# Centroids as 64 more columns of the weights in the first stage, and the third norm's parts of five late products kept in memory

## The chip, the core and the metric

The kernel runs on one core of a Trainium2 chip. TensorE multiplies, VectorE, ScalarE and GpSimd (POOL in the rows) do elementwise work, SyncE (SP) issues most DMAs, and 16 DMA engines move the data. The metric is the device time of one execution in microseconds.

## The reference

x has 4 x 1024 tokens of 1024 numbers. The computation is a macaron block:

```
x = x + 0.5 * ffn(layernorm(x))
x = x + attention(layernorm(x))
x = x + 0.5 * ffn(layernorm(x))

ffn(y):  dots = softmax(y @ centroids.T / 0.1)        # 64 clusters
         hits = dots > 0.01
         dense = y @ weight.T + bias                   # 1024 x 1024
         out = where(any(hits, 1)[:, None] & any(hits, 0)[assignments][None, :], dense, 0)
```

Both ffn use the same weight, bias, centroids and assignments. The attention mixes, within each token, 32 query heads with 8 key and value heads of width 32.

## The kernel before

**Tiles and precision.** The 4096 tokens are 32 tiles of 128 (NT = 32), two tiles form a pair (NP = 16). Every operand of a product is split into a high part (fp32r) and a low part (what the rounding left), and a product is three matmuls for each of 8 blocks of 128 inner columns: high x high, high x low weight, low x high weight (`product`, L280). One half of the outputs, 512 columns, is thus 24 matmuls into one bank of the accumulation memory; each matmul has its own weight load, since the tokens are the stationary side:

```
pe.matmul(acc, hi[:, k, :], w_h[:, k, cols], start=(k == 0), stop=False)
pe.matmul(acc, hi[:, k, :], w_l[:, k, cols], start=False, stop=False)
last = pe.matmul(acc, lo[:, k, :], w_h[:, k, cols], start=False, stop=(k == KB - 1))
```

The order of work is written out by hand: each engine has one program, and semaphores join them.

**First stage** (to about 390 us). It computes the first ffn's dense outputs and the logits. Per tile: statistics on VectorE (`stats_first`), factors on GpSimd (`factors_first`), the normalised tile on ScalarE (`norm_first`, L742). From tile 4 on it is stored to memory (`store_normed`, L406) and loaded back in four block DMAs (`load_blocks`, L410), so that VectorE's 32 x 32 transposes turn it fully (`turn_first`, L984). ScalarE copies the high part (`high_first`, L751) and VectorE subtracts the low part (`low_first`, L988, semaphore `lo1`). TensorE then makes two halves a tile (`product_first`), and VectorE adds the bias into `f_out` (`read_first`, L1000). GpSimd masks tokens (`select_tokens`), and SP stores the tile.

The logits of a pair come from a product of their own, the other way round: the centroids are stationary, the tokens of both tiles are 256 moving columns (`pair_logits`, L295, 16 matmuls; `pair_first`, L1293). ScalarE copies the result (`copy_pair`), TensorE transposes it in two matmuls inside a later product (`fold_pair`, L1302), and VectorE adds its parts and makes the softmax (`pair_soft_in` L332, `pair_soft_out` L352, with the exponential on ScalarE between). TensorE's loop over the pairs 1 to 13 is: first half of tile 2p with the fold of pair p inside, second half, centroid product of pair p + 1, both halves of tile 2p + 1. Pairs 14 and 15 follow, and the mask of the output columns is made from all hits.

**Stage of attention** (to about 1010 us). Iteration i works on several tiles at once: projections of tile i - 1, scores of tile i - 2, heads of tile i - 3, the third norm of tile i - 4 with its transposes on TensorE, high copy (`high_third`, L874) and low part (`low_third`, L1112), and a half product of the second ffn. The parts of the third norm lie in the two sets `odd_hi` and `odd_lo`, even and odd tiles. The values of a tile are loaded into the first half of the tile `part` and transposed by VectorE into the other.

**Last stage** (from about 1012 us). The products of the 14 tiles in `LATE` (tile 31, then 5, 7, ... 29; v counts them) had no room in the stage before. Since their third norm's parts were overwritten, they are made again for each v: load of the tile, `norm_late` (L855), 8 transposes (`transpose_late`, L1393), `high_late`, `low_late`, and then two halves (`product_late`, L1401) into banks that alternate by v. VectorE reads each half under the masks (`read_late`), adds it (`add_late`), and between them finishes 18 tiles whose products were done earlier (`finish_ready`, L1202); from the fourth on these come through three slots by DMA (`load_stream`, L568) and a mask multiplication on GpSimd (L737).

## Time and profile before

| | us |
|---|---|
| three runs | 1194.28, 1195.89, 1196.83 |
| median of the runs | 1195.89 |
| the profiled execution, own time | 1196.15 |
| its span | 1194.3 |
| TensorE busy in the span | 1181.7 |
| VectorE, ScalarE, GpSimd busy | 799.3, 499.2, 441.0 |

The page counts busy time of each engine; matmuls are pipelined and their ends modelled, so the starts of TensorE's instructions tell more than their lengths. A row of a timeline has start, length, engine, line, operation, output and input, and in brackets the idle time ahead of it and who ended it. The clock granted to TensorE was full in all stretches.

### The profile page before, as it was taken

To read this page: it belongs to the slowest core of one execution; us is meant where nothing else is said; L and a number is where in the kernel's file an instruction comes from. 1 tells how busy PE (TensorE), PEld (TensorE's weight loads), DVE (VectorE), ACT (ScalarE), POOL (GpSimd) and SP (SyncE) were. 2 spreads that over 40 slices of the span, in tenths; PEclk is the share of its full clock that TensorE was granted. 3 is DMA by queue.
4 is the path that set the end of the run, shared out by engine and by line. 5 is a ranking of instruction groups with operands and counts; after the bars stand their busy time and mean duration, and the time that the engine had idled before them with its cause. 6 is when DMAs were issued, how large, how long until landed. Compare 5 with 4: busy or idle time off the path is not lost.

```text
span 1194.3 us, 24986 instructions
## 1 busy us (share of the span) xinstructions
PE 1181.7 (99%) x10072; PEld 1002.5 (84%) x10072; DVE 799.3 (67%) x1272; ACT 499.2 (42%) x718; POOL 441.0 (37%) x582
## 2 busy tenths in 40 slices
PE   7999999999999999999999999999999999999998
PEld 6888888888888888888888888888888878888887
DVE  6654554455444477787777877778777774199987
ACT  5232233222211355656656656565565663211110
POOL 1335445543424643433434334344343210051332
PEclk9999999999999999999999999999999999999999
DMA  8578777876565366565565666565655565017885
GB/s 275 144 206 232 207 206 193 225 211 182 164 189 159 98 169 169 148 171 146 160 166 139 181 152 152 160 155 164 161 142 164 129 169 193 2 72 259 279 304 195
DMA packets 344978, 208.73 MB, mean 175 GB/s; under 512 B 289440, under 2 KB 308640, under 8 KB 344864
## 3 DMA queue, kind: packets, MB, share of 16 engines
q1 hardware_dynamic: 329696, 187.73, 56.2%
q10 hardware_dynamic: 15168, 19.40, 4.7%
q8 instruction: 80, 1.31, 0.5%
q14 instruction: 34, 0.28, 0.1%
HBM read 118.49 MB, written 88.60 MB: 173 GB/s over the span
## 4 chain that ended last, share of the span: by engine, by line
PE 91%; DMA 3%; DVE 2%; issue 1%; ACT 1%; SPq 1%; POOL 1%; POOLq 0%; DVEq 0%
PE ps_b L285 9%; PE ps_q L285 8%; PE ps_q L287 8%; PE ps_q L286 8%; PE ps_b L287 8%; PE ps_b L286 8%; PE ps_a L285 8%; PE ps_a L287 8%; PE ps_a L286 8%; PE ps_t L292 6%; PE ps_q L1450 3%; PE ps_q L299 2%; PE ps_q L301 2%; PE ps_q L1425 2%; DMA y_scratch<-xa 1%
## 5 line engine op out<-in xcount | busy, mean ns | idle before, releaser
L318 POOL TENSOR_TENSOR var_eps<-moments,eps 128x1 f32<-128x1 f32 x96 | 18.2, 190 | 396.6 <-DVE moments L314 396.6
L285 PE MATMUL ps_a<-w_hi,odd_hi 128*128 128x512 f32 x368 | 147.7, 401 | 0.0
L287 PE MATMUL ps_a<-w_hi,odd_lo 128*128 128x512 f32 x368 | 143.8, 391 | 0.0
L286 PE MATMUL ps_a<-w_lo,odd_hi 128*128 128x512 f32 x368 | 143.2, 389 | 0.0
L635 POOL TENSOR_SCALAR f_out<-f_out,token_on 128x1024 f32<-128x1024 f32 x30 | 85.6, 2852 | 75.6 <-DVE f_out L1013 75.3
L686 POOL TENSOR_TENSOR x_ring<-x_ring,f_tmp 128x1024 f32<-128x1024 f32 x32 | 77.3, 2414 | 91.2 <-DVE best L1159 58.5
L285 PE MATMUL ps_b<-proj_hi,y_hi 128*128 128x512 f32 x256 | 103.3, 403 | 0.0
L287 PE MATMUL ps_b<-proj_hi,y_lo 128*128 128x512 f32 x256 | 100.0, 391 | 0.0
L286 PE MATMUL ps_b<-proj_lo,y_hi 128*128 128x512 f32 x256 | 99.7, 390 | 0.0
L327 ACT ACTIVATE y_tok<-x_ring,norms 128x1024 f32<-128x1024 f32 x64 | 79.7, 1245 | 38.0 <-ACT o_head L881 21.0
L737 POOL TENSOR_TENSOR late<-late,mask 128x1024 f32<-128x1024 f32 x18 | 44.1, 2463 | 137.3 <-DMA late<-x_scratch 91.6
L1120 DVE TENSOR_TENSOR y_lo<-ps_t,y_hi 128x1024 fp32r<-128x1024 f32 x32 | 39.2, 1224 | 76.1 <-ACT y_hi L900 76.1
L893 ACT COPY v_diag<-part 32x256 f32<-32x256 f32 x128 | 82.7, 646 | 1.1
L287 PEld LDWEIGHTS ps_a<-w_hi,odd_lo 128*128 128x128 f32 x368 | 69.1, 188 | 15.1
L286 PEld LDWEIGHTS ps_a<-w_lo,odd_hi 128*128 128x128 f32 x368 | 69.3, 188 | 13.1
L285 PEld LDWEIGHTS ps_a<-w_hi,odd_hi 128*128 128x128 f32 x368 | 69.2, 188 | 12.7
L285 PE MATMUL ps_q<-w_hi,odd_hi 128*128 128x512 f32 (+1 forms) x208 | 79.5, 382 | 0.0
L287 PE MATMUL ps_q<-w_hi,odd_lo 128*128 128x512 f32 (+1 forms) x208 | 79.3, 381 | 0.0
L286 PE MATMUL ps_q<-w_lo,odd_hi 128*128 128x512 f32 (+1 forms) x208 | 79.3, 381 | 0.0
L285 PE MATMUL ps_q<-proj_hi,y_hi 128*128 128x256 f32 x256 | 74.8, 292 | 0.0
L287 PE MATMUL ps_q<-proj_hi,y_lo 128*128 128x256 f32 x256 | 72.5, 283 | 0.0
L286 PE MATMUL ps_q<-proj_lo,y_hi 128*128 128x256 f32 x256 | 72.4, 283 | 0.0
(219 smaller groups left out, 3113.1 us busy)
## 6 DMA issues: line engine op xcount, KB each, us to landing
xa<-in_L_attn_x SPq DMA_DIRECT2D x32, 512.0 KB, 5.0
f_tmp<-f_scratch SPq DMA_DIRECT2D x32, 512.0 KB, 4.2
x_ring<-in_L_attn_x SPq DMA_DIRECT2D x32, 512.0 KB, 3.6
f_scratch<-f_out SPq DMA_DIRECT2D x30, 512.0 KB, 4.0
x_scratch<-x_ring SPq DMA_DIRECT2D x30, 512.0 KB, 3.5
y_scratch<-xa SPq DMA_DIRECT2D x28, 512.0 KB, 4.6
ya_tok<-y_scratch SPq DMA_DIRECT2D x112, 128.0 KB, 3.3
late<-x_scratch SPq DMA_DIRECT2D x22, 512.0 KB, 6.7
```

Of the source, the lines that this page charges most:

```text
L285: pe.matmul(acc, hi[:, k, :], w_h[:, k, cols], start=(k == 0), stop=False)
L286: pe.matmul(acc, hi[:, k, :], w_l[:, k, cols], start=False, stop=False)
L287: last = pe.matmul(acc, lo[:, k, :], w_h[:, k, cols], start=False, stop=(k == KB - 1))
L292: last = pe.transpose(ps_t[:, k, :], src[:, k * P:(k + 1) * P], ident[:, :])
L299: last = pe.matmul(pair_ps, cen[:, k, :], hi[:, k, :, :], start=(k == 0), stop=(k == KB - 1))
L327: return act.activation(y, x, ACT.Identity, bias=norms[of][:, t, 0:1], scale=norms[of][:, t, 1:2])
L635: pool.tensor_scalar(f_out[t % 2][:, :], f_out[t % 2][:, :], token_on[0][:, t:t + 1], None, ALU.mult).then_inc(f1_on, 1)
L686: pool.tensor_tensor(x_ring[t % RING][:, :], x_ring[t % RING][:, :], f_tmp[:, :], ALU.add).then_inc(x1, 1)
L737: pool.tensor_tensor(f[:, :], f[:, :], mask[:, :], ALU.mult).then_inc(s_masked, 1)
L893: last = act.copy(v_diag[rows, :].rearrange("p (k q g c) -> p q k g c", k=R4, g=HKV, c=T4)[:, :, :, :, c], v_cols[rows, :].rearrange("p (q ...
L1120: dve.tensor_tensor(y2_lo[:, :, :], ps_t[:, :, :], y2_hi[:, :, :].bitcast(F32), ALU.subtract).then_inc(lo2, 1)
L1450: last = pe.matmul(scores_of[32 * c:32 * c + 32, r, :, j, :], q_head[rows, n * D:(n + 1) * D], k_mask[rows, n * P:(n + 1) * P].rearrange(" ...
```

## The change

It has two parts.

**Centroids as columns.** The weights' high part, the centroids' high part, the centroids' low part, the weights' low part and the centroids' low part once more lie side by side in one tile `w_all`; `w_hi` and `w_lo` are now 1088 columns wide. In pairs 1 to 13 the centroid product and the fold are gone. Each tile makes three pieces of 384, 352 and 352 columns (`product_wide`); the third holds 288 outputs and the 64 logits, and goes to a bank of its own. Both third pieces of a pair come first. VectorE reads the logits from there (`wide_soft_in`, one copy a tile), makes maximum and difference (`wide_soft_max`), and reads outputs in three pieces (`read_wide`). Pairs 0, 14 and 15 keep the old way.

**Parts in memory.** For the late products v = 3 to 7 (tiles 9 to 17) high and low part of the third norm are stored to memory in the stage of attention, where they are first made (`store_part`), and loaded in the last stage straight into the sets that the product reads (`load_parts`). Their norm, transposes, high copy and low part in the last stage are gone. The values of a tile get a tile `v_both` of their own, since `part` moved.

```diff
@@ constants and buffers @@
+WIDE = EMB + NCL
+PARTS = [slice(0, 384), slice(384, 736), slice(736, WIDE)]
...
+    WIDE_PAIRS = range(1, NP - 2)
     LATE = [LAST] + list(range(5, NT - 2, 2))
+    LOADED = list(range(3, 8))
+    TURNED = [v for v in range(1, len(LATE)) if v not in LOADED]
+    parts_d = nc.dram_tensor("parts_scratch", (len(LOADED), 2, P, KB, P), F32, kind="Internal").ap()
...
-        w_hi, w_lo = sb("w_hi", [P, KB, EMB], F32R), sb("w_lo", [P, KB, EMB], F32R)
-        cen = sb("cen", [P, KB, 2 * NCL], F32R)
+        w_all = sb("w_all", [P, KB, 2 * WIDE + NCL], F32R)
+        w_hi, cen, w_lo = w_all[:, :, 0:WIDE], w_all[:, :, EMB:EMB + 2 * NCL], w_all[:, :, WIDE + NCL:2 * WIDE + NCL]
...
+        def wide_bank(t):
+            return ps_q[:, 2 + t % 2, 0:WIDE - PARTS[2].start]
@@ VectorE, opening: centroids' low part, now twice @@
-                dve.tensor_tensor(cen[:, :, NCL:2 * NCL], cen_ps, cen[:, :, 0:NCL].bitcast(F32),
-                                  ALU.subtract).then_inc(cen_lo, 1)
+                for cen_low in (w_lo[:, :, EMB:WIDE], cen[:, :, NCL:2 * NCL]):
+                    dve.tensor_tensor(cen_low, cen_ps, w_hi[:, :, EMB:WIDE].bitcast(F32), ALU.subtract).then_inc(cen_lo, 1)
@@ VectorE, logits @@
+        def wide_soft_in(dve, u, n):
+            t = 2 * u + n
+            wait(dve, soft_exp, u)
+            dve.wait_ge(ffn1_wide, 16 + t - 1)
+            at = EMB - PARTS[2].start
+            dve.tensor_copy(pair_exp_in[:, n * NCL:(n + 1) * NCL], wide_bank(t)[:, at:at + NCL]).then_inc(soft_step, 1)
@@ SP, stage of attention and last stage @@
+                def store_part(v, n):
+                    sp.wait_ge(lo3, LATE[v] + 1)
+                    sp.dma_start(parts_d[LOADED.index(v), n], third_set(LATE[v])[n].bitcast(F32)).then_inc(parts_stored, 16)
...
+                    for n in range(2):
+                        if i - 4 - n in LATE[1:] and LATE.index(i - 4 - n) in LOADED:
+                            store_part(LATE.index(i - 4 - n), n)
...
+                def load_parts(v):
+                    n = LOADED.index(v)
+                    sp.wait_ge(parts_stored, Y_IN + 32 * n + 32)
+                    for h in range(2):
+                        sp.wait_ge(ffnl[h], v - 2)
+                    for m, part_of in enumerate(late_set(v)):
+                        sp.dma_start(part_of.bitcast(F32), parts_d[n, m]).then_inc(parts_in[n % 3], 16)
...
                 for v in range(NL):
                     if 7 <= v + 4 < NL:
                         load_late(v + 4)
+                    if v + 3 in LOADED:
+                        load_parts(v + 3)
@@ ScalarE, high part of the third norm @@
                 def high_third(t):
                     act.wait_ge(t3, t + 1)
+                    if t - 2 in LATE[1:] and LATE.index(t - 2) in LOADED:
+                        act.wait_ge(parts_stored, Y_IN + 32 * LOADED.index(LATE.index(t - 2)) + 32)
@@ TensorE, first stage @@
+                def product_wide(t, part, between={}):
+                    hi, lo = first_set(t)
+                    pe.wait_ge(lo1, t + 1)
+                    if part < 2:
+                        wait(pe, f1_read[part], t - 1)
+                        bank, done = first_bank(t, part)[:, 0:PARTS[part].stop - PARTS[part].start], ffn1[part]
+                    else:
...
+                        pe.wait_ge(soft_in, t // 2)
+                        wait(pe, wide_read, 16 + t - 3 if t > 3 else 0)
+                        bank, done = wide_bank(t), ffn1_wide
+                    product(pe, bank, hi, lo, w_hi, w_lo, PARTS[part], between).then_inc(done, 1)
@@ TensorE, late products @@
-                    if v + 1 < NL:
+                    if v + 1 in TURNED:
                         transpose_late(v + 1)
```

TensorE in pair 2 of the first stage, before: the first row of each product and, in between, the fold (L285 is the first matmul of `product`, L299 and L301 belong to the centroid product).

```order
L285 MATMUL ps_a<-w_hi,even_hi 128x512 [waits f1_read0,lo1]
...
L306 MATMUL ps_q<-ident,pair_sums 128x128 [waits pair_copied]
...
L285 MATMUL ps_q<-w_hi,even_hi 128x512 [waits f1_read1,lo1]
...
L299 MATMUL ps_q<-odd_hi,cen 128x256 [waits soft_in,pair_copied,lo1]
...
L285 MATMUL ps_b<-w_hi,even_hi 128x512 [waits f1_read0,lo1]
```

The same pair now, each row the first of 24 (L303 is L285, and the tile `w_all` holds the weights).

```order
L303 MATMUL ps_q<-w_all,even_hi 128x352 [waits w_in7,soft_in,lo1]
...
L303 MATMUL ps_a<-w_all,even_hi 128x384 [waits f1_read0,lo1]
...
L303 MATMUL ps_q<-w_all,even_hi 128x352 [waits f1_read1,lo1]
...
L303 MATMUL ps_b<-w_all,even_hi 128x384 [waits f1_read0,lo1]
...
L303 MATMUL ps_q<-w_all,even_hi 128x352 [waits f1_read1,lo1]
```

The centroid product and the fold are gone, and two pieces of 352 columns, one for each tile of the pair, stand at the front (the first row stands for both), waiting for the softmax input of the pair before.

VectorE in a pair of the first stage now, from the turn of tile 2p + 2 to the statistics of tile 2p + 5 (L1042 is the turn, L1047 the low part, L1078 `read_wide`, L328 the statistics; the six rows of the softmax's output are left out).

```order
L1042 STREAM_TRANSPOSE ya_tok0<-ya_tok0 128x1024 [waits y_in0]
L370 COPY pair_exp_in<-ps_q 128x64 [waits w_in6,soft_exp]
L1047 TENSOR_TENSOR odd_lo<-ya_tok0,odd_hi 128x8x128 [waits hi1]
...
L1078 TENSOR_TENSOR f_out0<-ps_q,bias_a 128x288 [waits f1_stored0,w_in6]
L375 TENSOR_REDUCE pair_max<-pair_exp_in 128x2 [waits soft_step]
...
L328 BN_STATS bn0<-xa2 128x6 [waits xa_in2]
...
L1042 STREAM_TRANSPOSE ya_tok1<-ya_tok1 128x1024 [waits y_in1]
...
L1047 TENSOR_TENSOR odd_lo<-ya_tok1,odd_hi 128x8x128 [waits hi1]
L328 BN_STATS bn1<-xa0 128x6 [waits xa_in0]
```

Before, the softmax's input, its output and the statistics all followed the first turn without a wait for a product of this pair; now the second copy of logits, for tile 2p + 1, stands between the low part and the statistics, and the output of the softmax has moved behind the second turn.

TensorE in the last stage, late products 2 and 3, before (L292 are transposes).

```order
L292 MATMUL ps_t<-ident,f_tmp 128x128 [waits lol,yl]
...
L285 MATMUL ps_a<-w_hi,y2_hi 128x512 [waits l_read0,lol]
...
L292 MATMUL ps_t<-ident,probs 128x128 [waits lol,yl]
...
L285 MATMUL ps_b<-w_hi,odd_hi 128x512 [waits l_read0,lol]
```

The same now.

```order
L303 MATMUL ps_a<-w_all,y2_hi 128x512 [waits l_read0,lol]
...
L303 MATMUL ps_q<-w_all,y2_hi 128x512 [waits l_read1,lol]
...
L303 MATMUL ps_b<-w_all,odd_hi 128x512 [waits l_read0,y_in1]
```

The transposes for products 3 and 4 are gone, and product 3 waits for the load of its parts (`y_in1`) in place of the low part (`lol`).

## Rows read from the trace of the kernel before

**Rows 1.** The page: the chain that ended last, by engine

```profile
PE 91%; DMA 3%; DVE 2%; issue 1%; ACT 1%; SPq 1%; POOL 1%; POOLq 0%; DVEq 0%
```

**Rows 2.** Stretches: busy us (instructions) per engine, clock, DMA share, GB/s

```profile
300.00:400.00 100.00, 100.00 (x486) 83.05 (x485) 45.09 (x93) 19.24 (x23) 43.39 (x43) 1.00 0.56 163
...
1061.50:1073.30 11.80, 11.80 (x58) 9.83 (x57) 11.66 (x10) 2.16 (x2) 4.76 (x2) 1.00 0.33 134
```

**Rows 3.** Timeline of TensorE, last tile: start, length, instruction

```profile
1179.38 0.39 PE L285 MATMUL ps_b<-w_hi,odd_hi 128*128 128x512 f32 x1
...
1184.82 0.28 PE L285 MATMUL ps_q<-w_hi,odd_hi 128*128 128x256 f32 x1
...
1190.45 0.28 PE L287 MATMUL ps_q<-w_hi,odd_lo 128*128 128x256 f32 x1
```

**Rows 4.** Timeline of TensorE, pair 13 of the first stage

```profile
336.20 0.39 PE L285 MATMUL ps_a<-w_hi,odd_hi 128*128 128x512 f32 x1
...
341.90 0.39 PE L285 MATMUL ps_q<-w_hi,odd_hi 128*128 128x512 f32 x1
...
347.34 0.28 PE L299 MATMUL ps_q<-even_hi,cen 128*128 128x256 f32 x1
...
349.20 0.40 PE L285 MATMUL ps_b<-w_hi,odd_hi 128*128 128x512 f32 x1
```

**Rows 5.** Timeline of VectorE, pair 9: last read-outs and statistics

```profile
240.54 0.69 DVE L1013 TENSOR_TENSOR f_out<-ps_q,bias_a 128x512 f32<-128x512 f32 x1 [4.75 <-PE ps_q L287]
...
245.96 0.69 DVE L310 BATCH_NORM_STATS2 bn<-xa 128x6 f32<-128x512 f32 x1
...
264.47 0.69 DVE L1013 TENSOR_TENSOR f_out<-ps_q,bias_a 128x512 f32<-128x512 f32 x1 [4.75 <-PE ps_q L287]
```

**Rows 6.** Timeline of ScalarE, pair 13: normalisation of tiles 30 and 31

```profile
345.50 1.24 ACT L327 ACTIVATE xa<-xa,norms 128x1024 f32<-128x1024 f32 x1
...
349.58 1.24 ACT L327 ACTIVATE xa<-xa,norms 128x1024 f32<-128x1024 f32 x1 [2.84 <-POOL norms L323]
```

**Rows 7.** Timelines of VectorE and TensorE in the opening

```profile
19.49 1.39 DVE L997 TENSOR_TENSOR w_lo<-ps_q,w_hi 128x512 fp32r<-128x512 f32 x2 [0.92 <-ACT w_hi L760]
...
83.89 0.38 PE L299 MATMUL ps_q<-odd_hi,cen 128*128 128x256 f32 x1 [1.07 <-DVE odd_lo L991]
```

**Rows 8.** Timeline of SP, block loads of tile 30

```profile
351.27 3.98 SPq L422 DMA_DIRECT2D ya_tok<-y_scratch  x4
```

**Rows 9.** Timeline of VectorE, turn of tile 30, low part of tile 31

```profile
357.66 1.25 DVE L986 STREAM_TRANSPOSE ya_tok<-ya_tok 128x1024 f32<-128x1024 f32 x1 [2.08 <-DMA ya_tok<-y_scratch]
...
364.84 1.23 DVE L991 TENSOR_TENSOR odd_lo<-ya_tok,odd_hi 128x1024 fp32r<-128x1024 f32 x1 [1.12 <-ACT odd_hi L755]
```

**Rows 10.** Timeline of TensorE, centroid product of pair 15

```profile
367.18 0.28 PE L299 MATMUL ps_q<-odd_hi,cen 128*128 128x256 f32 x1
```

**Rows 11.** Page, two DMA issues; ScalarE and TensorE in the stage of attention

```profile
x_scratch<-x_ring SPq DMA_DIRECT2D x30, 512.0 KB, 3.5
...
late<-x_scratch SPq DMA_DIRECT2D x22, 512.0 KB, 6.7
...
596.88 1.25 ACT L327 ACTIVATE y_tok<-x_ring,norms 128x1024 f32<-128x1024 f32 x1
...
598.46 1.04 PE L292 MATMUL ps_t<-ident,y_tok 128*128 128x128 f32 x8
```

**Rows 12.** Timeline of TensorE, transposes for late products 4 and 10

```profile
1061.48 1.04 PE L292 MATMUL ps_t<-ident,probs 128*128 128x128 f32 x8
...
1132.22 1.04 PE L292 MATMUL ps_t<-ident,probs 128*128 128x128 f32 x8
```

**Rows 13.** Timelines of VectorE and TensorE in the last stage

```profile
1071.10 0.74 DVE L1193 SCALAR_TENSOR_TENSOR part<-ps_a,token_on,mask 128x512 f32<-128x512 f32 x1
...
1074.08 0.48 PE L285 MATMUL ps_a<-w_hi,odd_hi 128*128 128x512 f32 x1
...
1186.44 1.28 DVE L1211 SCALAR_TENSOR_TENSOR late<-k_mask,token_on,late 128x1024 f32<-128x1024 f32 x1 [3.40 <-POOL late L737]
```

More of the change, by code:

```diff
@@ L128, in macaron_kernel @@
             y2_hi, y2_lo = sb2("y2_hi", [P, KB, P], F32R), sb2("y2_lo", [P, KB, P], F32R)
+            with ExitStack() as later:
+                part = later.enter_context(nc.sbuf_tensor("part", [P, EMB], F32))
             qkv_tok = sb2("qkv_tok", [P, PROJ])
@@ L134, in macaron_kernel @@
             probs = sb2("probs", [P, EMB])
-            part = sb2("part", [P, EMB])
+            v_both = sb2("v_both", [P, 2 * HD])
             x_ring.append(sb2(f"x_ring{RING - 1}", [P, EMB]))
@@ L788, in _ @@
                 act.wait_ge(cen_t, 1)
-                act.copy(cen[:, :, 0:NCL], cen_ps).then_inc(cen_hi, 1)
+                act.copy(w_hi[:, :, EMB:WIDE], cen_ps).then_inc(cen_hi, 1)
                 high_rows(8)
@@ L815, in _ @@
                         high_proj(p - 2)
-                    copy_pair(p + 1)
+                    if p + 1 not in WIDE_PAIRS:
+                        copy_pair(p + 1)
                 high_first(NT - 2)
@@ L964, in _ @@
                 for v in range(3, NL):
-                    high_late(v)
+                    if v in TURNED:
+                        high_late(v)
                     if v == 3:
                         store_late(0)
-                    if v + 1 < NL:
+                    if v > 3 and v + 1 in TURNED:
                         norm_late(v + 1)
@@ L1014, in read_first, with read_wide @@
                                           ALU.add).then_inc(f1_read[h], 1)
+                def read_wide(t, part):
+                    cols = PARTS[part] if part < 2 else slice(PARTS[2].start, EMB)
+                    done, bank, by = ((ffn1[part], first_bank(t, part), f1_read[part]) if part < 2 else
+                                      (ffn1_wide, wide_bank(t), wide_read))
+                    dve.wait_ge(done, t + 1 if part < 2 else 16 + t - 1)
+                    wait(dve, f1_stored[t % 2], 16 * (t // 2))
+                    dve.tensor_tensor(f_out[t % 2][:, cols], bank[:, 0:cols.stop - cols.start], bias_a[:, cols],
+                                      ALU.add).then_inc(by, 1)
                 dve.memset(best[0][:, :], 0.0)
@@ L1056, in _ @@
                 low_first(3)
-                for p in range(1, NP - 2):
-                    read_first(2 * p - 1, 1)
+                for p in WIDE_PAIRS:
+                    if p == 1:
+                        read_first(1, 1)
+                    else:
+                        read_wide(2 * p - 1, 1)
                     turn_first(2 * p + 2)
-                    pair_soft_in(dve, p)
+                    wide_soft_in(dve, p, 0)
                     low_first(2 * p + 2)
-                    pair_soft_out(dve, 0, p)
+                    wide_soft_in(dve, p, 1)
+                    read_wide(2 * p, 2)
+                    wide_soft_max(dve, p)
                     stats_first(2 * p + 4)
                     turn_first(2 * p + 3)
-                    read_first(2 * p, 0)
+                    pair_soft_out(dve, 0, p)
+                    read_wide(2 * p, 0)
+                    read_wide(2 * p + 1, 2)
                     low_first(2 * p + 3)
                     stats_first(2 * p + 5)
-                    read_first(2 * p, 1)
-                    read_first(2 * p + 1, 0)
+                    read_wide(2 * p, 1)
+                    read_wide(2 * p + 1, 0)
                 turn_first(NT - 2)
@@ L1075, in _ @@
                 low_first(LAST)
[L1076 removed]
+                read_wide(NT - 5, 1)
                 read_first(NT - 4, 0)
@@ L1336, in _ @@
                 product_first(1, 1)
-                pair_first(1)
-                for p in range(1, NP - 2):
-                    product_first(2 * p, 0, {3 if p == 1 else 1: lambda: fold_pair(p)})
-                    product_first(2 * p, 1)
-                    if p > 1:
-                        pair_first(p + 1)
-                    product_first(2 * p + 1, 0)
-                    if p == 1:
-                        pair_first(p + 1)
-                    if p < NP - 3:
-                        product_first(2 * p + 1, 1)
-                product_first(NT - 5, 1, {1: lambda: fold_pair(NP - 2)})
+                for p in WIDE_PAIRS:
+                    product_wide(2 * p, 2)
+                    product_wide(2 * p + 1, 2)
+                    product_wide(2 * p, 0)
+                    product_wide(2 * p, 1)
+                    if p + 1 not in WIDE_PAIRS:
+                        pair_first(p + 1)
+                    product_wide(2 * p + 1, 0)
+                    product_wide(2 * p + 1, 1, {} if p + 1 in WIDE_PAIRS else {1: lambda: fold_pair(NP - 2)})
                 product_first(NT - 4, 0)
```

70 lines of the change are left out of this document (46 added, 24 removed).

## The prediction

> **What bounds the kernel.** The page's chain comes first: 91% of the work that ended last is TensorE's [rows 1]. The stretches say the same of both places that change: in the first stage (300 to 400 us) and the last (one tile from 1061.5 us) TensorE never pauses at the full clock, while VectorE is busy 45% and 99% of the time [rows 2]. So the time is a sum of TensorE's own spacings, as long as nobody makes it wait. Its timeline prices them. In the last tile 24 matmuls of 512 columns take 1184.82 - 1179.38 = 5.44 us, 226.7 ns each, and 48 of 256 columns (47 spacings) 5.63 us, 119.8 ns each [rows 3]. Durations in the rows (390, 280 ns) overlap and are not used. In pair 13 (tiles 26 and 27) a product with the fold inside takes 5.70 us, so a fold costs 0.26 us, and the centroid product of a pair 1.86 us [rows 4].
>
> **First stage, TensorE.** A pair took 264.47 - 240.54 = 23.93 us [rows 5]. Now a tile takes 24 matmuls in each of three column pieces, 384, 352 and 352, and 13 pairs lose centroid product and fold. No row shows 384 or 352 columns. The line through the two known widths is (226.7 - 119.8) / 256 = 0.4176 ns a column plus 12.9 ns a matmul, so 173.3 and 159.9 ns. A tile is 24 x (0.1733 + 2 x 0.1599) = 11.83 us, a pair 23.67 us, 0.26 us less than before: 13 x 0.26 = **3.4 us gained**. It is a small difference of large numbers: 1872 narrow matmuls replace 1248 wide ones, so 1 ns on each is 1.9 us. Bounds: if a narrow matmul costs in proportion to the 512 row (170.0 and 155.9 ns), a tile is 11.56 us and 26 tiles give 7.0 us more; in proportion to the 256 row (179.7 and 164.7 ns) a tile is 12.22 us and 10.1 us are lost against the line. I take the line, since both widths lie between its ends.
>
> The Trainium skill (TensorE: Matmul & The Clock Gate, section Back-to-back issue gap) has columns / 2.4 + 2.5 ns for a spacing, which would make a tile 11.06 us and leave the third piece nearly free. By that the stage would gain over 9 us. The rows disagree on the fixed part: they have 11 to 13 ns beyond columns / 2.4 [rows 3].
>
> **First stage, who feeds TensorE.** The pieces with the logits of both tiles now stand at the front of a pair, and VectorE can finish a pair's softmax input only after both (7.7 us into the pair). Behind that wait stand the statistics of tile 2p+4, which before began 245.96 - 240.54 = 5.4 us after the last read [rows 5] and now begin about 9.1; the turn of tile 2p+3 and its low part follow (end about +15.1). Nothing else on VectorE grows: the logit path loses one add of 0.3 us and the read-outs get one more start. TensorE needs that low part only 3.8 us into the next pair, at +27.5, so 12 us cover it in the middle of the stage. Behind it on other queues: ScalarE's normalisation of tile 2p+4 ends at +14.1 where it ended at 345.50 + 1.24 - 336.20 = +10.5 [rows 4, 6]; SP's store and the block loads follow it and land about when the turn wants them, at +24.3. VectorE may wait a little there; TensorE does not.
>
> Two places have less cover. **Opening:** TensorE waited 1.07 us for the low part of tile 7, [rows 7], because the centroid product wanted it at once. The new order wants it about 9 us later in the chain, so **1.1 us are gained**. The extra low part of the centroids is one more start on VectorE near 18 us, and 0.92 us of waiting for ScalarE follows it at 19.49 [rows 7]: it costs nothing. **End of the stage:** the normalisations of tiles 30 and 31 ended 10.5 and 14.6 us into pair 13, their stores went out then, the four block loads of tile 30 were issued from 351.27 to 355.25 [rows 6, 8], VectorE waited 2.08 us for them and turned at 357.66, and the low part of tile 31 ended at 364.84 + 1.23 = 366.07, 1.1 us before the centroid product of pair 15 started at 367.18 [rows 9, 10]. Now the two normalisations end at +14.1 and +19.0. The loads land at +25.7, and the same 8.4 us from turn to low part give +34.1. TensorE arrives there after four pieces (15.68), centroid product (1.87), a piece (4.20), a piece with the fold (4.10), a product (5.44) and six matmuls (1.36): +32.7. **1.4 us are lost**, between 0 and 3.
>
> **Stage of attention.** Ten stores of 512 KB are added, at most two an iteration, at the end of SP's iteration. ScalarE's next write of the same high part now waits for the stores of the tile that held it, issued most of an iteration earlier; transfers of this size land in 3.5 to 6.7 us [rows 11]. A wait would count, since the second norm on ScalarE comes right behind that write, from 596.88 to 598.13, and TensorE's transposes start at 598.46 [rows 11], 0.3 us later. An iteration lasts over 17 us, so I cost it at nothing; uncovered, it would be what the store lands late, five times. The value tile of its own removes no wait.
>
> **Last stage.** Late products 3 to 7 lose their 8 transposes, the high copy, the low subtraction and the norm. One tile with transposes takes (1132.22 - 1061.48) / 6 = 11.79 us [rows 12], two products alone 2 x 5.44 = 10.88, so 0.91 us each and **5 x 0.91 = 4.55 us gained**, provided that TensorE stays the bound. VectorE: per tile it loses 1.2 us while TensorE loses 0.91, so its lag does not grow. The tightest place is late product 4, which may start (1074.08) once the read-out of product 2 (1071.10, 0.74 us) has freed the bank [rows 13]: 2.2 us of cover. It gains 2.4 us from the two low parts ahead of it (3 and 4) and loses 1.8, so the cover stays. The loads of the parts (1 MB each) are issued one and a half to two products ahead, some 12 to 20 us; DMA is 33% busy there [rows 2]. The last 38 us keep their order: last low parts, masks, VectorE waiting 3.4 us for GpSimd's mask behind a load [rows 13], which hangs on tiles 11 and 12 and moves with them.
>
> **Sum.** 3.4 + 1.1 - 1.4 + 4.55 = 7.65 us off. The profiled execution took 1196.15 us with a span of 1194.3; the median of the runs is 1195.89, 0.26 lower. 1196.15 - 7.65 = 1188.5, less 0.26: **1188.2 us**.
>
> **Rivals.**
> - *Columns only.* A matmul costs in proportion to its columns, the fixed part being hidden: 1188.2 - 7.0 = 1181.2 us. Against it: 256 columns cost more than half of 512 [rows 3]. The rule of the Trainium skill (same page and section) points this way. 7%.
> - *Narrow matmuls cost more (slower).* Place: all 72 matmuls of each of 26 tiles. Each piece now needs its own weight load, 72 a tile for 48, under shorter matmuls; if a 352- or 384-column matmul costs as many ns a column as one of 256 does, the stage loses 6.7 us in place of gaining 3.4, and the time is 1188.2 + 10.1 = 1198.3 us. It turns the sign once a narrow matmul costs over 4 ns more than the line. Against it: loads hide under 256 columns at 119.8 ns. 7%.
> - *The last stage pays nothing.* The loads of 5 MB join streams that already make VectorE wait for masks [rows 13]; VectorE falls behind and TensorE waits for banks, so the 4.55 us come back: 1192.7 us. For it: VectorE is busy 11.66 of 11.80 us before the change [rows 2]; against: it sheds more than TensorE. 12%.
> - *The feed of the first stage paces it.* The later normalisations make the turns late by more each pair, until the 12 us are used up; at 0.5 us a pair, 6.5 us are lost: 1194.7 us. Against: everything hangs on TensorE's own pace and catches up within a pair. 6%.
>
> **Numbers.** The forecast keeps 68%. Its own spread is 1.5 ns on a narrow matmul (2.8 us), 0 to 3 us for the wait at the end of the first stage, and 1 us in the last: 1184 to 1192. The range 1182.5 to 1193.5 adds the third rival and part of the first. A measurement of this kernel can tell about 0.2% (2.4 us) from no change, so faster means below 1193.5: forecast, first and third rival, less their upper tails, 0.84. The fourth rival and those tails give 0.09 for the same, the second 0.07 for slower.
>
> **What would show it.** Right: spacings of 173 and 160 ns; 23.67 us between the read-outs of two pairs; no wait at 84 us; a wait of about 1.4 us on VectorE's low part before the centroid product of pair 15; late tiles 10.9 us apart five times, then 11.8. Wrong: spacings over 164 ns at 352 columns, TensorE waiting inside pairs 2 to 12, ScalarE waiting for a store before it copies the third norm's high part, or a wait for a bank or a part in the last stage.

## The result and the profile after

The changed kernel took 1198.08 us (median of 7 runs, 1196.1 to 1200.95), the kernel before 1194.97 on the same chip: a ratio of 1.0028 with a 95% interval of 1.0015 to 1.0040. It is slower by 0.3%, and the prediction of 1188.2 with a range of 1182.5 to 1193.5 was wrong in sign. The profiled execution has a span of 1196.1 us, 1.8 more than before; the medians differ by 3.1 us, so the traces hold a little over half of the loss.

The page of the changed kernel: span, busy time of the engines, transfers, one queue (packets, MB, share), and the chain that ended last.

```profile
span 1196.1 us, 25786 instructions
...
PE 1175.4 (98%) x10422; PEld 1046.9 (88%) x10422; DVE 794.5 (66%) x1294; ACT 485.0 (41%) x695; POOL 443.5 (37%) x582
...
DMA packets 363990, 219.27 MB, mean 183 GB/s; under 512 B 289760, under 2 KB 327392, under 8 KB 363872
...
q8 instruction: 83, 1.36, 0.5%
...
PE 83%; DVE 6%; DMA 4%; issue 3%; SPq 1%; POOL 1%; ACT 0%; POOLq 0%; DVEq 0%
```

TensorE's share of the chain fell from 91% [rows 1] to 83%; VectorE, DMA and "issue" took it. TensorE is busy 6.3 us less than before in a longer span. Two things are new: time in which TensorE waits for nothing that the profile names, and an end that belongs to VectorE.

**The first stage came as predicted.** TensorE's timeline of pair 3, first matmul of each piece:

```profile
93.45 0.32 PE L303 MATMUL ps_q<-w_all,odd_hi 128*128 128x352 f32 x1
...
101.06 0.34 PE L303 MATMUL ps_a<-w_all,odd_hi 128*128 128x384 f32 x1
...
105.25 0.32 PE L303 MATMUL ps_q<-w_all,odd_hi 128*128 128x352 f32 x1
...
109.11 0.34 PE L303 MATMUL ps_b<-w_all,odd_hi 128*128 128x384 f32 x1
...
113.28 0.32 PE L303 MATMUL ps_q<-w_all,odd_hi 128*128 128x352 f32 x1
...
117.14 0.32 PE L303 MATMUL ps_q<-w_all,even_hi 128*128 128x352 f32 x1
```

48 matmuls of 352 columns take 7.61 us (158.5 ns each), 24 of 384 take 4.17 to 4.19 (174 ns), a pair 117.14 - 93.45 = 23.69 us. The wait at 84 us [rows 7] is gone, and pair 15's centroid product waits 0.54 us:

```profile
363.59 0.38 PE L317 MATMUL ps_q<-odd_hi,w_all 128*128 128x256 f32 x1 [0.54 <-DVE odd_lo L1047]
...
384.15 1.03 PE L310 MATMUL ps_t<-ident,y_tok 128*128 128x128 f32 x8
```

The second row is the first transposition of the stage of attention. Before, it stood at 387.65: 3.50 us gained. One pair of traces is a rough measure of this: the same row stands at 386.10 to 390.06 us in the four traces with the old first stage, and at 384.10 to 385.59 in the nine wide ones without waits ahead of everything. What all traces share is the spacing of the pairs of tiles, 23.93 us before and 23.69 now, 3.1 us in 13 pairs.

**The stage of attention lost 5.2 us.** Lining the two timelines of TensorE up product by product, every product there takes the same in both traces to 0.05 us, but for three places. The small matmuls of a tile (two groups of 64, 1.7 us in all) stand ahead of each:

```profile
436.60 0.76 PE L1514 MATMUL ps_q<-probs,v_diag 128*32 128x32 f32 x64
437.29 0.50 PE L303 MATMUL ps_b<-proj_hi,y_hi 128*128 128x512 f32 x1
...
439.33 0.39 PE L304 MATMUL ps_b<-proj_lo,y_hi 128*128 128x512 f32 x1 [0.86 <-issue]
...
787.97 0.76 PE L1514 MATMUL ps_q<-probs,v_diag 128*32 128x32 f32 x64
790.96 0.39 PE L303 MATMUL ps_b<-proj_hi,y_hi 128*128 128x512 f32 x1 [2.23 <-issue]
...
974.97 0.76 PE L1514 MATMUL ps_q<-probs,v_diag 128*32 128x32 f32 x64
...
977.13 0.39 PE L303 MATMUL ps_b<-w_all,y_hi 128*128 128x512 f32 x1
979.64 0.50 PE L304 MATMUL ps_b<-w_all,y_hi 128*128 128x512 f32 x1 [2.12 <-issue]
...
980.44 0.63 PE L304 MATMUL ps_b<-w_all,y_hi 128*128 128x512 f32 x1
980.87 0.63 PE L305 MATMUL ps_b<-w_all,y_lo 128*128 128x512 f32 x1
981.29 0.63 PE L303 MATMUL ps_b<-w_all,y_hi 128*128 128x512 f32 x1
```

They cost 1.0, 2.2 and 4.0 us. At the last, eight matmuls behind the pause start 0.43 us apart, not 0.227 (the last three rows are among them): TensorE had paused 2.1 us, and the granted clock fell to the lower of its two levels (1.2 of 2.4 GHz; mean 0.89 from 970 to 986 us) for 3.4 us, worth 1.6 of the 4.0. The kernel before pauses at one place only, and shorter; its product there takes 6.72 us:

```profile
982.69 0.50 PE L285 MATMUL ps_b<-w_hi,y_hi 128*128 128x512 f32 x1 [0.85 <-issue]
```

So 1.0 + 2.2 + (4.0 - 1.2) = 6.0 us are lost, 0.8 come back in small steps, and the last stage begins 1.7 us later than before: -3.5 + 6.0 - 0.8.

**The last stage took as long as before.** I measure it on VectorE from its first read behind the mask to its last add; before:

```profile
1045.31 0.75 DVE L1193 SCALAR_TENSOR_TENSOR part<-ps_a,token_on,mask 128x512 f32<-128x512 f32 x1 [5.16 <-ACT mask L390]
...
1191.72 0.42 DVE L1253 TENSOR_TENSOR late<-late,part 128x256 f32<-128x256 f32 x1
```

and in the changed kernel, with VectorE's two longest waits, and the SyncE and GpSimd rows behind the first:

```profile
1047.02 0.75 DVE L1267 SCALAR_TENSOR_TENSOR part<-ps_a,token_on,mask 128x512 f32<-128x512 f32 x1 [5.16 <-ACT mask L423]
...
1110.15 1.28 DVE L1285 SCALAR_TENSOR_TENSOR late<-k_mask,token_on,late 128x1024 f32<-128x1024 f32 x1 [7.28 <-POOL late L789]
...
1188.22 1.28 DVE L1285 SCALAR_TENSOR_TENSOR late<-k_mask,token_on,late 128x1024 f32<-128x1024 f32 x1 [2.78 <-POOL late L789]
...
1193.50 0.42 DVE L1324 TENSOR_TENSOR late<-late,part 128x256 f32<-128x256 f32 x1
```

```profile
1093.07 0.52 SPq L628 DMA_DIRECT2D odd_hi<-parts_scratch  x1
1093.63 1.93 SPq L628 DMA_DIRECT2D odd_lo<-parts_scratch  x1
1095.61 3.01 SPq L634 DMA_DIRECT2D out<-late  x1
1098.72 1.06 SPq L614 DMA_DIRECT2D late<-f_scratch  x1
1099.82 0.94 SPq L615 DMA_DIRECT2D late<-x_scratch  x1
...
1107.97 2.15 POOL L789 TENSOR_TENSOR late<-late,mask 128x1024 f32<-128x1024 f32 x1 [7.73 <-DMA late<-x_scratch]
```

146.8 us before, 1193.92 - 1047.02 = 146.9 now. TensorE itself did what was forecast: late products 3 to 7 are 10.88 us apart (in a stretch of one, 1062.29 to 1073.18, it is busy 10.89 us, VectorE 10.79, for 11.80 and 11.66 in [rows 2]), the transposes of one late tile wait 0.50 us for VectorE's low part (at 1118.27 us), and its last matmul starts at 1188.33 for 1190.45. But VectorE ends 5.6 us behind it, for 1.7 before.

### The profile page after: what moved, and what is told of

It is laid out like the page before. It is cut to its first block, busy times and chain, and to the rows that moved or that the text cites. A ratio compares the mean times of both kernels' runs of the same rounds, so it can differ in the third digit from the quotient of the medians.

```text
span 1196.1 us, 25786 instructions
## 1 busy us (share of the span) xinstructions
PE 1175.4 (98%) x10422; PEld 1046.9 (88%) x10422; DVE 794.5 (66%) x1294; ACT 485.0 (41%) x695; POOL 443.5 (37%) x582
## 3 DMA queue, kind: packets, MB, share of 16 engines
q8 instruction: 83, 1.36, 0.5%
## 4 chain that ended last, share of the span: by engine, by line
PE 83%; DVE 6%; DMA 4%; issue 3%; SPq 1%; POOL 1%; ACT 0%; POOLq 0%; DVEq 0%
PE ps_q L303 9%; PE ps_q L305 9%; PE ps_q L304 9%; PE ps_b L303 8%; PE ps_b L304 7%; PE ps_b L305 7%; PE ps_a L303 7%; PE ps_a L305 7%; PE ps_a L304 7%; PE ps_t L310 5%; PE ps_q L1539 3%; DMA late<-x_scratch 2%; PE ps_q L1514 2%; PE ps_q L317 1%; PE ps_q L319 1%
## 5 line engine op out<-in xcount | busy, mean ns | idle before, releaser
L303 PE MATMUL ps_a<-w_all,odd_hi 128*128 128x512 f32 (+1 forms) x368 | 143.8, 391 | 0.0
L305 PE MATMUL ps_a<-w_all,odd_lo 128*128 128x512 f32 (+1 forms) x368 | 140.6, 382 | 0.0
L304 PE MATMUL ps_a<-w_all,odd_hi 128*128 128x512 f32 (+1 forms) x368 | 140.2, 381 | 0.0
L303 PE MATMUL ps_q<-w_all,odd_hi 128*128 128x352 f32 (+2 forms) x320 | 108.1, 338 | 0.0
L305 PE MATMUL ps_q<-w_all,odd_lo 128*128 128x352 f32 (+2 forms) x320 | 107.8, 337 | 0.0
L304 PE MATMUL ps_q<-w_all,odd_hi 128*128 128x352 f32 (+2 forms) x320 | 107.6, 336 | 0.0
L303 PE MATMUL ps_b<-proj_hi,y_hi 128*128 128x512 f32 x256 | 102.9, 402 | 2.2 <-issue 2.2
L949 ACT COPY v_diag<-v_both 32x256 f32<-32x256 f32 x128 | 82.5, 645 | 1.1
L305 PEld LDWEIGHTS ps_a<-w_all,odd_lo 128*128 128x128 f32 x368 | 69.1, 188 | 12.8
L304 PEld LDWEIGHTS ps_a<-w_all,odd_hi 128*128 128x128 f32 x368 | 69.3, 188 | 11.1
L303 PEld LDWEIGHTS ps_a<-w_all,odd_hi 128*128 128x128 f32 x368 | 69.2, 188 | 10.9
L303 PE MATMUL ps_q<-proj_hi,y_hi 128*128 128x256 f32 x256 | 74.8, 292 | 0.0
L303 PE MATMUL ps_q<-w_all,even_hi 128*128 128x352 f32 (+1 forms) x224 | 74.6, 333 | 0.0
L305 PE MATMUL ps_q<-w_all,even_lo 128*128 128x352 f32 (+1 forms) x224 | 74.3, 332 | 0.0
```

The lines of the kernel that those rows point to most:

```text
L949: last = act.copy(v_diag[rows, :].rearrange("p (k q g c) -> p q k g c", k=R4, g=HKV, c=T4)[:, :, :, :, c], v_cols[rows, :].rearrange("p (q ...
```

## The experiments

The first reading of the pauses was one of two: A, they come with TensorE's instruction stream; B, they come with the added transfers. And for the last stage: the parts' loads on SyncE's queue (C), or VectorE and the tiles streamed to it (E).

**The two halves apart, the change again, and a mended last stage.** The first:

```diff
-    LOADED = list(range(3, 8))
+    LOADED = []
```

with the calls of `norm_late`, `low_late` for late products 3 and 4 as before. The second keeps `LOADED` and has before's loops over the pairs (`WIDE_PAIRS` empty). The fourth, the mended kernel, moves `load_parts` into ScalarE's loop and swaps two calls on SyncE:

```diff
+                        if 3 <= k - 1 and k + 2 < len(READY):
+                            load_stream(k + 2)
                         store_ready(k)
-                        if 3 <= k - 1 and k + 2 < len(READY):
-                            load_stream(k + 2)
```

> The first stage of the change alone: centroids as 64 more columns, all late products still turned on TensorE, no parts stored or loaded. In the changed kernel the products of the stage of attention started 3.50 us earlier than before (388.44 against 391.94), and 5.2 us were lost again by 1027 us, in three pauses of TensorE that no semaphore explains (1.0 us at 437, 2.2 at 789, 4.0 against 1.2 before at 976). Theory A, the pauses come with TensorE's own instruction stream (in each, a block of instructions was being fetched), whose blocks begin elsewhere because the first stage now has 400 more instructions pairs: the pauses stay in some form, and the time is 1195.0 - 3.5 + (0 to 5) = 1191.5 to 1196.5 us, with pauses at 437 or 789 us in the trace. Theory B, the ten stores of parts (5 MB more to memory) delay the fetches: no pause but the one at 976 of before, 1191.5 us. The last stage must look as before: last VectorE instruction 1.3 us behind the last matmul.

> The second half of the change alone: before's first stage, parts of late products 3 to 7 stored and loaded. Theory A (pauses by the place of instruction blocks, which is as before until the last stage): products at 437 and 789 us run without a pause, only the one of before at 976 (1.2 us). Theory B (pauses by the stores): pauses of 1 to 2 us after 600 us, where the stores are, none at 437. In the last stage both expect what the changed kernel showed: TensorE gains 3.8 us, the loads of parts and the stores of finished tiles on SyncE's queue delay the stream, VectorE idles some 9 us between 1097 and 1110, and ends 5.5 us behind TensorE, so that only 0 to 1 us are left: 1194 to 1195 by A, 1197 to 1199 by B, against 1195.0 before. My prediction's own terms would give 1195.0 - 4.55 = 1190.4.

> The changed kernel once more, for a second trace of it. If the pauses at 437, 789 and 976 us belong to the program (Theory A), they come back at the same products, perhaps with other lengths; if they are chance (a fetch that happens to meet other transfers), they stand elsewhere. The time: 1197 to 1199.

> The changed kernel with two edits to the order of issues in the last stage: the loads of parts are issued by ScalarE (behind its stores of late tiles) in place of SyncE, and SyncE issues the two loads of stream tile k+2 ahead of the store of finished tile k, not behind it. Nothing is computed otherwise. Theory C, the last stage loses its gain because the loads of parts stand ahead of stores and stream loads on SyncE's queue and the stream loads hang on VectorE's last finished tile: VectorE's waits for GpSimd's masks at 1098 to 1110 us (9.3 us) and at 1185 (2.8 us) go, VectorE ends 1 to 4 us behind TensorE, and the time falls by 3 to 5 us from the changed kernel's 1198: 1193 to 1195. Rival D, VectorE itself is too slow (its work per tile and the 3 us instructions under GpSimd's): less than 1 us is gained.

Measured, as ratios to before with intervals: the wide first stage alone 1.0001 (0.9989 to 1.0013), parts alone 1.0001 (0.9989 to 1.0013), the change again 1.0028 (1.0015 to 1.0042), mended 1.0015 (1.0000 to 1.0031). Each half alone changes nothing that can be told; parts did not gain my 4.55 us. The pauses: the change again has them at the same three products (1.2, 2.8, 1.9 us idle), the mended kernel too (0.5, 2.6, 1.3), the wide stage alone at the first and last (1.0, 2.4) and not at 790 us, parts alone only where before has one (0.2). So they belong to the program, as A says, and the one at 790, where parts are being stored, seemed to need the stores as well. Of the last stage, mended takes 143.9 us for 146.9; by this one trace C looked right, though its ratio cannot be told from the changed kernel's.

Counting places in the compiled program settled where they stand. TensorE's list has 20605 instructions before and 21316 in the change, 64 bytes each, which is the 1.36 MB of queue q8; in its 83 packets a packet is 16.4 KB, 256 instructions. The place is the instruction's number, counted from 0, less the full multiples of 256. For each pause, the first matmul behind it:

```
kernel               at us    instruction   of 256
before               982.69   18377         201
changed              439.33    5832         200
changed              790.96   14536         200
changed              979.64   19145         201
changed again        439.71    5832         200
changed again        792.28   14536         200
changed again        982.57   19145         201
wide stage alone     440.75    5832         200
wide stage alone     981.06   19145         201
```

A matmul at 201 has its weight load at 200. Every pause is thus at the first instruction of a block of 256, and always close behind (or in) a tile's 128 small matmuls, which are 256 instructions in 1.7 us. A block is used up there faster than the next one comes. The change puts 796 instructions, 3 x 256 + 28, ahead of the stage of attention, so that all places there move by 28.

The packets of queue q8 show it from the other side. One takes 0.9 to 2.6 us. Fifteen of the traces have waits of this kind, 26 in all, every one at place 200 or 201, and in each a packet ends 1.2 to 1.6 us before TensorE goes on. At 790 us TensorE runs through the small matmuls, from one border to the next, in 1.7 us if nothing stops it. Counted from the first matmul behind the earlier border, in us:

| kernel | packet starts | packet ends | idle at the next border |
|---|---|---|---|
| changed | 1.29 | 2.52 | 2.23 |
| changed again | 2.27 | 3.23 | 2.83 |
| mended | 2.02 | 2.98 | 2.63 |
| stream order alone (below) | 1.55 | 2.51 | 2.10 |
| relieved (below) | 1.11 | 2.31 | 2.04 |
| wide stage alone, no parts stored | -0.87 | 0.02 | none |
| before with a shift of 28 (below), no parts stored | -0.79 | 0.63 | none |

So the pause is the wait for the block, and with the stores of parts the block came later. In the changed kernel one of them, of `odd_lo`, is issued at 783.15 us, 3.8 us ahead of the earlier border; from 4 us ahead of that border to 1 us behind it the DMA share is 0.98 to 1.04 in the five traces with stores, 0.90 and 0.92 in the other two. Whether it is these bytes that hold the packet up was not separated. A pause also varies from one execution to the next: at 440 us six traces with these places paused, with the packet's end 2.0 to 2.8 us behind the border, and the stream order alone did not, with 1.3 us.

The Trainium skill (Runtime: NRT & Kernel Launch, section Instruction fetch mechanics) has the 16 KiB blocks and calls the cost of crossing one mostly hidden. By this case it is so for all but at most three of the 80 to 84 blocks of a trace; those that show are in or behind such groups.

**Only the places moved.** Waits on a semaphore that is long set stand ahead of TensorE's first work; the build puts two into one instruction:

```diff
+                for _ in range(56):
+                    pe.wait_ge(const_set, 1)
                 pe.wait_ge(ident_set, 2)
```

> The kernel before with 56 waits on a semaphore that is long set, ahead of TensorE's first work (two to an instruction, so 28 instructions; TensorE is idle there until 5.7 us). Nothing else. Reading so far: TensorE's program is fetched in blocks of 256 instructions (queue q8 of the profile: 1.36 MB in 83 packets, for 21316 instructions of 64 bytes). In every pause without a releaser, in three traces of two programs, the first matmul behind it is instruction 200 or 201 of 256: a block begins there. A pause comes where that place falls within some 20 instructions behind the 128 small matmuls (256 instructions in 1.7 us) of a tile of attention. The change moved every later instruction by 28 places of 256. Theory A: this kernel gets the changed kernel's places, and so its pauses: about 1 us in the product at 439 us and 3 to 4 us in the product at 977 (1.2 before), 2 to 4 us slower than before: 1198 to 1200. The pause at 790 comes only if no stores of parts are needed for it: 0 to 2 us. Rival B (pauses come from the first stage's or the stores' other traffic): no change, 1196.

> The changed kernel with 104 such waits (52 instructions). By the compiled program the nearest block borders behind a tile's small matmuls are then 10, 18 and 30 instructions away, at the 26th, 7th and 2nd tile, and the one at 976 us is 220 away. Theory A: no pause at 437, 790 and 976 us; at most a small new one near 900 us; 4 to 6 us less work to wait for TensorE, but the last stage is bound by VectorE from the mask on, so all of it is passed on to the end: 1199 - 5 = 1194 to 1196. Rival B: as the changed kernel, 1198 to 1200.

> The two edits of the last stage (parts loaded from ScalarE's queue, stream loads ahead of the store) with the same shift of 52 instructions. If both causes are right and add up: the last stage from the mask to the last VectorE instruction takes 144 us as in the repaired kernel (147 before and in the changed one), and the pauses are gone: 1190.5 to 1193 us, faster than before by 3 to 5 us. If only the order of the last stage counts: 1198.

> The first stage of the change alone with the same shift. Theory A: no pause at 437 and 976; before lost 1.2 us at 976. So before minus the first stage's gain (3.4 us less 0.4 to 1.5 in its opening and end) minus 1.2: 1191 to 1193.5 us. Rival B: 1196, as without the shift.

The kernel before, given the changed kernel's places, shows its pauses:

```profile
442.14 0.39 PE L286 MATMUL ps_b<-proj_lo,y_hi 128*128 128x512 f32 x1 [0.64 <-issue]
...
981.36 0.50 PE L286 MATMUL ps_b<-w_lo,y_hi 128*128 128x512 f32 x1 [2.84 <-issue]
```

at instructions 5064 and 18377, places 200 and 201; the product at 977 takes 10.32 us for 6.72, and there is none at 790, where this kernel stores no parts. Its time is 1.0011 of before (0.9999 to 1.0022): 1.3 us slower by the ratio and 2.0 by the medians, where A said 2 to 4, and by the time alone not certain. The changed kernel with places moved by 52 lost its three pauses and fell to 0.9996 (0.9983 to 1.0008), about 4 us less; the wide stage alone to 0.9979 (0.9968 to 0.9990). B is out as the cause of the place; by the table above, the stores can still make a block late. I had overlooked borders a few instructions ahead of a group: the next one then falls inside it, and the changed kernel paused there, at 717.87 (1.4 us idle, the weight load is instruction 12744, place 200). The mended kernel with the shift gave 0.9999 (0.9988 to 1.0011), not the 3 to 5 us forecast: 2.0 us idle at 718 with a slow clock behind it, and 145.9 us for the last stage. The waits ahead of everything also cost 1.2 us: TensorE started at 7.0 us, not 5.8.

**The shift where it is hidden, at equal places, and VectorE relieved.** In the wide kernel two met waits (one instruction) went ahead of each of the first 52 pieces, in the kernel before 80 instructions ahead of products of the same stage, to the same places:

```diff
+                    if 3 * (t - 2) + (part + 1) % 3 < 52:
+                        pe.wait_ge(const_set, 1)
+                        pe.wait_ge(ident_set, 2)
```

> The first stage of the change alone, with the same shift of 52 instructions, but as two met waits (one instruction) ahead of each of the first 52 column pieces in place of 104 waits ahead of everything: there they took 1.2 us (TensorE began at 7.0 us for 5.8). Theory A: no pause in the stage of attention, and the first stage hides the waits behind its matmuls: 1193.8 - 1.2 = 1192 to 1193 us, before less 3 to 4 us. If TensorE pays for each wait, the first stage grows by what the opening showed, 1.2 us, and nothing is gained over the other shift.

> The kernel before with 80 instructions of met waits spread over the first stage's products, which gives it the very block places of the kernel with the shift of 52. Its pause at 977 us (1.2 us) goes, none comes: 1195 to 1195.5 for 1196.2. Beside it the wide first stage shows what it is worth at equal places: by my prediction 3.4 us less what its end loses, so 2 to 3.4 us. If the wide columns themselves bring nothing, both kernels take the same.

> The changed kernel, but for late products 3 to 7 the bias is added to one column of 1024 (so these five tiles lack the bias elsewhere): VectorE loses five instructions of 1.2 us in the last stage, TensorE nothing. Theory E, VectorE and the loads that hang on it set the last stage, not TensorE: the time from the mask to the last VectorE instruction falls from 146.9 to 141 to 144 us, and the whole by 3 to 5 us from the changed kernel's 1199. Rival F, TensorE or the transfers alone set it: less than 1 us.

The wide stage reached 0.9970 (0.9960 to 0.9980), 1190.72 us; before at its places 1.0001 (0.9991 to 1.0011), 1194.13 us. At equal places the wide columns are worth 3.4 us (the latter has 28 more instructions of waits). TensorE came to the stage of attention at 385.31 us, for 385.42 without the shift and after 0.9 us less of waiting, so the 52 cost under 1 us there. By the ratios with their intervals the difference is 3.7 us, give or take 1.7. The loss of the pause at 977 did not show in before's time: it got one of 1.0 us at 720 in its place (the wide kernel has one of 0.7 at 715), and TensorE's wait at 84 us was 1.9 us in that trace, with 3.4 us at the lower clock behind it. The relieved kernel is the changed one with the bias of late products 3 to 7 added on one column of 1024, so that it leaves most of their bias out. It took 1.0006 (0.9994 to 1.0017) for the changed kernel's 1.0028: 2.6 us less. Its profiled execution took 4094 us and is not read.

**What sets the last stage, and whether parts pay anywhere.** The stream half of the mended kernel alone, the relieved kernel for a trace, and both candidates with 74 instructions of shift:

> The changed kernel with one of the two edits of the repaired one: SyncE issues the loads of stream tile k+2 ahead of the store of finished tile k; the loads of parts stay on SyncE. In the repaired kernel the stretch from the mask to the last VectorE instruction was 143.9 us, for 146.9 in the changed one. If the stream order did it, this kernel shows 144 to 145 too, with the 9 us wait of VectorE between 1098 and 1110 us still there and the last waits (2.8 us at 1188) shorter, and 2 us less than the changed kernel's 1.0028 of before. If the parts' loads did it: 147.

> The kernel with the bias on one column for late products 3 to 7, for a trace: Theory E, VectorE with its masks and loads sets the last stage: 141 to 145 us from the mask to VectorE's last instruction, for 146.9; the time 1.000 to 1.001 of before, as in its first runs. If the 6 us taken from VectorE turn into longer waits for GpSimd's masks, so that the stretch stays above 146, then the stream of loads and stores sets it.

> The whole change with the repaired last stage and 74 instructions of met waits spread over the wide pieces; nearest block borders at 4, 8 and 9 instructions, at 548, 454 and 733 us. If both repairs hold: no pause over 1 us but perhaps one at 733, where the parts are stored (1 to 2 us), and 144 us for the last stretch: 1188 to 1191 us. If parts are worth nothing beside the wide stage: 1191 to 1194, no better than the kernel below.

> The wide first stage alone at the same places. The shift of 52 gave 0.997 of before with one pause of 0.9 us left, at 715. Here none over 0.5 us is expected, and a price of 0.5 us for 22 more waits: 0.9965 to 0.997 of before.

Ratios: 1.0037 (1.0022 to 1.0052), 0.9992 (0.9980 to 1.0003), 0.9965 (0.9952 to 0.9977), 0.9958 (0.9945 to 0.9972). The last stage in the traces, from VectorE's first read behind the mask to its last add:

| kernel | last stage, us | behind TensorE's last matmul, us | waits for GpSimd, us |
|---|---|---|---|
| before | 146.8 | 1.7 | 9.7 |
| wide stage alone, four traces | 146.4 | 1.3 | 8.8 to 9.3 |
| parts alone | 147.2 | 5.8 | 16.3 |
| changed, and again | 146.9, 147.1 | 5.6, 4.5 | 16.2, 17.5 |
| changed, shift 52 | 145.8 | 4.6 | 15.7 |
| stream order alone | 147.8 | 6.7 | 19.8 |
| mended: plain, shift 52, 74 | 143.9, 145.9, 146.5 | 3.3, 5.3, 5.9 | 15.5, 19.5, 17.9 |
| relieved | 143.7 | 3.1 | 14.1 |

C is not borne out: the stream order alone gains nothing, and the 143.9 us of the mended kernel did not come back in its two other traces. The parts' loads on ScalarE's queue with the old stream order were not run, so that half of C was never tested by itself. E holds in part: taking five instructions of 1.2 us from VectorE shortened the stage by 3.2 us in one trace, and the mended kernel's three traces already differ by 2.6; the time fell by 2.6 and 4.3 us in the two series (1.0006 and 0.9992 for 1.0028), and that carries the reading. The rest is in the last column: with parts, VectorE waits 14.1 to 19.8 us for masks, for 8.8 to 9.8 without, and the masks wait for the streamed tiles. Which transfer holds those up most was not separated.

**The best version** is the wide first stage alone with 74 instructions of shift: 1192.17 us for 1196.54 before, 0.9958 (0.9945 to 0.9972); it cannot be told from the 0.9970 with 52. All that TensorE still waits for, by its table of waits:

```profile
PE ps_a L1345 <- DMA w_raw<-in_L_ffn_weight: 5.7, 1, 5.7
PE ps_q L317 <- DVE odd_lo L1048: 1.3, 1, 1.3
PE ps_a L303 <- DVE w_all L1054: 0.7, 1, 0.7
PE ps_b L303 <- issue: 0.4, 1, 0.4
PE ps_q L317 <- DVE odd_lo L1188: 0.2, 1, 0.2
```

With parts at the same places (0.9965) it is no faster, though TensorE's last matmul starts 4.8 us earlier, and its last stage took 146.5 us where 144 were expected. Without pauses worth the name, parts gain nothing.

## Why the prediction was wrong

- **First stage, 3.4 us: right, by its mechanism.** 158.5 to 161 ns at 352 columns and 174 at 384, for 159.9 and 173.3 from the line; a pair 23.69 us for 23.67, which makes 3.1 us. At equal places the kernels differ by 3.4 us, with the waits of both first stages in it. The columns-only rival is out: 12 to 14 ns stand beyond columns / 2.4 (in [rows 3] it was 13, not the 11 to 13 that I wrote). The rival of dear narrow matmuls is out too, although the time it gave (1198.3) is nearly the one measured: by luck, since the mechanism was another. The columns-only rule in the Trainium skill (TensorE: Matmul & The Clock Gate, section Back-to-back issue gap) has 2.5 ns for the fixed part; the section calls that the gap of an isolated matmul, which I left out when I applied it to a stream with a weight load for each matmul. In this stream the trace has the 12 to 14 ns.
- **Opening, 1.1 us: right in kind.** The wait for tile 7's low part stood in two of four traces with the old first stage (1.07 and 1.93 us; a third had 0.8 us of such a wait at 275 us) and in none of the twelve wide ones. I took its size from one trace; it varies.
- **End of the stage, 1.4 us lost, 0 to 3: right.** 0.54 us in the changed kernel's trace and 0.7 to 3.3 in the eleven other wide ones; in seven of these a wait of pair 14's centroid product is in it, which I had not foreseen, and the longest, 3.3 us, is beyond my bound of 3.
- **Stage of attention, costed at nothing: the step that failed.** I looked for ScalarE waiting on stores, which did not come, and took TensorE's other work there as untouched. It was, but its place in the instruction stream was not: 28 places of 256 moved borders of blocks behind the small matmuls of three tiles. This cost 5.2 us net in the trace. The stores of parts, costed at nothing too, had a share: with them the pause at 790 stood in all five traces with these places (2.0 to 2.8 us idle), without them in neither of two, and the block's packet ended 2.3 to 3.2 us behind the earlier border for 0.0 and 0.6. Nothing in my sum or rivals had it, though before's trace had a row of its kind that I did not read: the wait on "issue" at 982.69 us.
- **Last stage, 4.55 us: wrong, and the failing step was "provided that TensorE stays the bound".** TensorE's part was right (10.88 us apart, 3.8 us earlier). I argued that VectorE sheds 1.2 us a tile where TensorE sheds 0.91, so that its lag cannot grow. But of the 6.1 us that it shed, 3.6 became longer waits (12.6 to 16.2 us in all) and 2.6 slower instructions, some of which take 3 us in place of 1.3 while GpSimd works (eight of at least 2.8 us, for five before); VectorE's chain had hardly any slack before: of its 12.6 us of waits in the stage only 0.5 were for a matmul, and with all of VectorE's work and the parts loaded by SyncE the stage takes 145.8 to 147.8 us in every trace. My third rival, the last stage pays nothing (1192.7 us, 12%), is what happened here, and masks behind loads are in it; that TensorE waits for banks, as it says, is not: VectorE ends late instead.
- **Sum.** By the trace: -3.5 (first stage with its ends) + 6.0 - 0.8 (attention) + 0.1 (last stage) = +1.8 us in the span, for -7.65 forecast. The other 1.3 us between the medians are not in these two traces and stay open.

## What to carry to other kernels

A group of very small matmuls can run through a whole fetched block of instructions faster than the next one arrives, so a change that only adds instructions far ahead can bring or take pauses of 1 to 4 us later; look for waits on "issue" in the timeline, and compare two versions at equal places before judging an edit worth a few us. Met waits spread over a long stage of matmuls move the places almost for free. Work taken from the engine that bounds a stage is a gain only up to the next chain: measure the stage from its first to its last instruction on every engine, not by the busiest one.

## What the runs showed of the hardware

- A block of instructions took longer to come than a tile's small matmuls run: at the waits its packet ended 1.0 to 6.1 us behind the first matmul of the block before, and TensorE went on 1.2 to 1.6 us after the packet's end in all 26 waits. From a group's start to the end of its pause passed 3.4 to 4.1 us at 437 and 4.8 to 7.6 at 975 us. The farthest behind a group that a block was still late was 44 instructions, at 977 us in the kernel before.
- A pause of about 2 us and more is sometimes followed by seven or eight matmuls of 512 columns at the lower clock (0.43 us apart): behind 2.12 us at 979.64 in the changed kernel, 2.83 at 792.28 in its second trace and 1.78 at 979.85 in the one with the stream order alone, but not behind 2.23 us at 790.96 in the first. It makes such a pause nearly twice as dear.
- Why blocks begin at place 200 of the compiled list and not at 0 stays open; it was the same in all kernels.
